# Loading and splitting the expert weights in ten 512 KB pieces, later in the prologue

## The reference, cut to what matters

```python
q, k, v = (split_heads(x @ w.T) for w in (wq, wk, wv))
attn = softmax(where(causal, q @ k.T * 8 ** -0.5, -inf))
x = layernorm(x + (attn @ v) @ wo.T)
coef = route(sigmoid(x @ router_w.T) + e_bias)        # top 4 of 8 groups, top 8 experts
g, u = einsum('th,ehi->tei', x, Wg), einsum('th,ehi->tei', x, Wu)
h = silu(g) * u * coef[:, :, None]
moe = einsum('tei,eih->th', h, Wd)
x = layernorm(x + moe + silu(x @ SWg) * (x @ SWu) @ SWd)
```

## Time and profile before

| | |
|---|---|
| median of three runs | 1035.29 us (1033.92 to 1036.24) |
| the profiled execution | 1035.23 us, of which its span is 1033.2 us |
| PE | 936.0 us busy, 91% of the span |
| DVE, POOL, ACT | 810.7, 626.7, 462.3 us busy (78%, 61%, 45%) |
| mean DMA rate | 117 GB/s over the span; 344 GB/s from 5 to 20 us |
| first matmul of the main loop | 137.41 us |

### The profile page before, as it was taken

How to read it: one execution, slowest core, us unless ns; L and a number is a source line. 1 busy time by engine, 2 the same in 40 slices (tenths; PEclk the granted TensorE clock), 3 DMA queues, 4 the chain that set the end, 5 groups by cost and what they waited for, 6 DMA issues and landing times.

```text
span 1033.2 us, 15722 instructions
## 1 busy us (share of the span) xinstructions
PE 936.0 (91%) x4800; PEld 564.4 (55%) x4800; DVE 810.7 (78%) x2435; ACT 462.3 (45%) x882; POOL 626.7 (61%) x668
## 2 busy tenths in 40 slices
PE   2687699999999899999999899999999999988996
PEld 1233356665566556665566556665566556655653
DVE  5765767798978997799977997798977986587554
ACT  2354345444444444445444444444444545433332
POOL 2432137665676556675676556675676667765775
PEclk7588689999999999999999999999999999999998
DMA  8441153332533253323533253322533232322331
GB/s 297 144 142 49 35 177 109 116 106 103 173 106 116 94 177 110 116 84 124 173 106 116 88 175 118 116 76 103 195 91 116 95 100 83 112 75 84 102 123 51
DMA packets 63075, 120.75 MB, mean 117 GB/s; under 512 B 7056, under 2 KB 34576, under 8 KB 62608
## 3 DMA queue, kind: packets, MB, share of 16 engines
q1 hardware_dynamic: 62992, 119.76, 36.0%
HBM read 97.32 MB, written 22.02 MB: 116 GB/s over the span
## 4 chain that ended last, share of the span: by engine, by line
PE 63%; DVE 27%; issue 4%; DMA 3%; POOL 2%; ACT 1%; SPq 0%; POOLq 0%; DVEq 0%
PE acc L594 8%; DVE max_out L890 7%; PE ob L541 7%; PE sm L511 5%; PE pu L472 5%; PE pg L472 5%; PE st L529 5%; PE pg L474 4%; PE pg L473 4%; PE pu L474 4%; PE pu L473 4%; DVE hid L963 4%; DVE hid L954 3%; PE acc L584 3%; PE acc L586 2%
## 5 line engine op out<-in xcount | busy, mean ns | idle before, releaser
L706 POOL TENSOR_TENSOR hid<-hid,coef_b 128x512 f32<-128x512 f32 x256 | 332.2, 1298 | 197.1 <-DVE hid L963 182.8
L655 ACT ACTIVATE hid<-pg 128x512 f32<-128x512 f32 x264 | 157.7, 597 | 359.9 <-PE pg L474 358.6
L890 DVE CUSTOM_DVE_ANT_0 max_out<-sm,causal_sb 128x128 bf16<-128x128 f32 (+3 forms) x512 | 235.6, 482 | 90.7 <-PE sm L511 89.3
L954 DVE SCALAR_TENSOR_TENSOR hid<-hid,pg 128x512 f32<-128x512 f32 x264 | 180.2, 682 | 86.9 <-ACT hid L655 86.9
L710 POOL TENSOR_TENSOR hid_lo<-hid,hid_hi 128x512 fp32r<-128x512 f32 x128 | 164.2, 1283 | 71.3 <-ACT hid_hi L662 70.0
L627 ACT ACTIVATE probs<-st 128x512 f32<-128x512 f32 (+1 forms) x384 | 187.1, 526 | 20.4 <-PE st L529 18.5
L963 DVE TENSOR_TENSOR hid<-hid,pu 128x512 f32<-128x512 f32 x256 | 174.6, 682 | 10.9 <-PE pu L474 6.2
L511 PE MATMUL sm<-k_stack,q_stack 72*128 72x128 bf16 (+3 forms) x512 | 140.9, 323 | 32.3 <-DMA k_stack<-k_rows_dram 16.5
L692 POOL TENSOR_SCALAR_AFFINE_SELECT probs<-probs 128x256 f32<-128x256 f32 x256 | 102.8, 426 | 75.4 <-ACT probs L627 74.9
L472 PE MATMUL pg<-x_hi,wg_hi 128*128 128x512 f32 x256 | 139.6, 545 | 9.8 <-DVE hid L954 9.7
L472 PE MATMUL pu<-x_hi,wu_hi 128*128 128x512 f32 x256 | 125.0, 488 | 15.7 <-DVE hid L963 15.6
(11 more groups left out here) (129 smaller groups left out, 1213.1 us busy)
## 6 DMA issues: line engine op xcount, KB each, us to landing
coef_b<-coef_dram SPq DMA_DIRECT2D x128, 512.0 KB, 3.9
q_rows_dram<-qk_parts SPq DMA_DIRECT2D x24, 384.0 KB, 3.3
k_rows_dram<-qk_parts SPq DMA_DIRECT2D x24, 384.0 KB, 3.7
q_stack<-q_rows_dram SPq DMA_DIRECT2D x64, 144.0 KB
k_stack<-k_rows_dram SPq DMA_DIRECT2D x64, 144.0 KB
xT_sb<-in_xT SPq DMA_DIRECT2D x8, 256.0 KB, 3.9
y<-in_x SPq DMA_DIRECT2D x8, 256.0 KB, 4.4
out<-out_sb SPq DMA_DIRECT2D x8, 256.0 KB, 2.4
```

Of the source, the lines that this page charges most:

```text
L706: pool.tensor_tensor(hid[:, i % 3, :], hid[:, i % 3, :], coef_b[:, half % 2, j, :], ALU.mult)\
L890: last = dve.tensor_tensor_reduce(out=max_out[:, seg.nth(BANK_SM, task) % 2, col:col + wide], in0=sm_of(seg, task)[:, col:col + wide], in1 ...
L954: dve.scalar_tensor_tensor(hid[:, i % 3, :], hid[:, i % 3, :], 1.0, pg[:, :], ALU.add, ALU.mult).then_inc(a_done, 1)
```

## The change

All weight pieces but SWgu are now quarters of 512 KB and pass through the two halves of coef_b; probs stages nothing any more. The order of the ten is g, u, d, g, u, g, u, d, g, u. Loads stand at places 4.4, 6.1, 7.8 and so on to 21.4, and each split 2.0 places behind its load. DVE computes only the low part of SWgu; POOL does all ten others. wd_sb leaves the group of small weights and is loaded right behind the last piece, with a semaphore that only the first matmul that reads it waits for.

```diff
-SPLIT_BY_DVE = 3
-CHUNKS = 9
+SPLIT_BY_DVE = 1
+CHUNKS = 11
...
-WEIGHT_LOADS = (-4.9, -4.25, -0.25, 2.9, 5.15, 6.8, 8.95, 12.6, 15.45)
-WEIGHT_SPLITS = (-0.09, 2.02, 5.9, 6.7, 9.05, 9.15, 10.1, 15.9, 16.8)
+WEIGHT_LOADS = tuple(4.4 + 1.7 * i for i in range(CHUNKS))
+WEIGHT_SPLITS = tuple(at + 2.0 for at in WEIGHT_LOADS)
...
-        wide, narrow = E * I // 2, E * I // 4
-        waiting = probs[:, :, :].rearrange("p h c -> p (h c)")
+        narrow = E * I // 4
-                  (Wg[:, 0:wide], wg_hi[:, 0:wide], wg_lo[:, 0:wide], waiting[:, 0:wide], 1),
-                  (Wu[:, 0:wide], wu_hi[:, 0:wide], wu_lo[:, 0:wide], waiting[:, wide:2 * wide], 2)]
-        for src, hi, lo, parts in ((Wg, wg_hi, wg_lo, (2, 3)), (Wu, wu_hi, wu_lo, (2, 3)), (Wd, wd_hi, wd_lo, (0, 1))):
+        g, u, d = (Wg, wg_hi, wg_lo), (Wu, wu_hi, wu_lo), (Wd, wd_hi, wd_lo)
+        for (src, hi, lo), part in ((g, 0), (u, 0), (d, 0), (g, 1), (u, 1), (g, 2), (u, 2), (d, 1), (g, 3), (u, 3)):
+            cols, half = slice(part * narrow, (part + 1) * narrow), (len(chunks) - 1) % 2
+            chunks.append((src[:, cols], hi[:, cols], lo[:, cols],
+                           coef_flat[:, half * narrow:(half + 1) * narrow], 1 + half))
...
-                 (sd_sb, SWd), (wd_sb, Wd[:, PAIRS // 2 * D:])]
+                 (sd_sb, SWd)]
...
+                        if i == CHUNKS - 1:
+                            sp.dma_start(wd_sb[:, :], Wd[:, PAIRS // 2 * D:]).then_inc(wd_in, 16)
...
+                            if (n, i) == (0, 2):
+                                pe.wait_ge(wd_in, 16)
```

More of the change, by code:

```diff
@@ L322, in build @@
         wq_in, wkv_in = sem("wq_in"), sem("wkv_in")
-        w_in = sem("w_in")
+        w_in, wd_in = sem("w_in"), sem("wd_in")
         id_in = sem("id_in")
-        split_in = [sem(f"split_in{j}") for j in range(5)]
+        split_in = [sem(f"split_in{j}") for j in range(3)]
         hi_done = sem("hi_done")
@@ L330, in build @@
         const_done = sem("const_done")
-        wide, narrow = E * I // 2, E * I // 4
-        waiting = probs[:, :, :].rearrange("p h c -> p (h c)")
+        narrow = E * I // 4
         coef_flat = coef_b[:, :, :, :].rearrange("p a j t -> p (a j t)")
-        chunks = [(SWgu, sgu_hi[:, :], sgu_lo[:, :], hid[:, 0, 0:2 * P], 0),
-                  (Wg[:, 0:wide], wg_hi[:, 0:wide], wg_lo[:, 0:wide], waiting[:, 0:wide], 1),
-                  (Wu[:, 0:wide], wu_hi[:, 0:wide], wu_lo[:, 0:wide], waiting[:, wide:2 * wide], 2)]
-        for src, hi, lo, parts in ((Wg, wg_hi, wg_lo, (2, 3)), (Wu, wu_hi, wu_lo, (2, 3)), (Wd, wd_hi, wd_lo, (0, 1))):
[L341 to L344, removed]
+        chunks = [(SWgu, sgu_hi[:, :], sgu_lo[:, :], hid[:, 0, 0:2 * P], 0)]
+        g, u, d = (Wg, wg_hi, wg_lo), (Wu, wu_hi, wu_lo), (Wd, wd_hi, wd_lo)
[3 more added lines that the diff above has]
+                           coef_flat[:, half * narrow:(half + 1) * narrow], 1 + half))
         assert len(chunks) == CHUNKS
         small = [(wo_sb, woT), (rw_sb, rwT), (bias_sb, bias.unsqueeze(0).to_broadcast([P, E])),
-                 (sd_sb, SWd), (wd_sb, Wd[:, PAIRS // 2 * D:])]
+                 (sd_sb, SWd)]
         block = ctx.enter_context(nc.Block())
```

## The result

| | before | after |
|---|---|---|
| median of the runs, us | 1034.61 (1033.92 to 1036.24) | 1045.49 (1044.70 to 1046.65) |
| span of the profiled execution, us | 1033.2 | 1043.5 |
| first maxima matmul | 21.14 | 19.57 |
| first `st` | 38.21 | 36.00 |
| second `pv` | 67.47 | 72.19 |

After takes 1.0104 times the time of before, 95% interval 1.0086 to 1.0121: slower by 1%. The row of medians rests on four runs of each kernel. Beside the later experiments, with 16 to 29 runs of before each time, before's median was 1036.6 to 1037.4, and against those the loss would be 8 to 9 us and not 10.9.

The account below looks back on a forecast made before the run. PE bounds the main loop, so its start, set by changing limits in the prologue, decides. Terms -4.1 + 0.4 + 4.5 + 0.3 + 6.5 + 1.1 = +8.7 us on 1035.23 give 1043.9 us, range 1034.5 to 1048.5.

Parts of the forecast that it names:

- rs 1.0: First row load of sequence 1: PE waits for it behind piece 10 and wd_sb; cost 6.5 us (2.4 to 7.2).
- heads 4 to 7: Prologue: POOL's low parts hold the k split and head 7's mask, and rs 0.6 lands later; cost 4.5 us.
- The opening: Start to the first st: weight megabyte off the first rows' path, less DVE work; gain 4.1 us (3.2 to 5.0).
- The rival by which the opening gives only 2 us: Stores limited by something else, so the megabytes stay on the path: 1046 us, inside the range, no chance of its own.
- Heads 0 to 3: Prologue after the first st: low part of piece 4 falls on mn's first step; cost 0.4 us (0 to 1).
- Heads 8 to 11: Prologue: ACT's high part of piece 8 overfills its gap and one st waits; cost 0.3 us.
- The clock: The pv behind the wait for rs 1.0 runs at PE's lower clock; cost 1.1 us (0 to 2.2).
- One for one: Main loop: nothing the change touches runs there, so any prologue gain or loss should pass whole to the end.
- row loads pass the weight loads: Rival at rs 1.0: weight loads don't hold it, PE waits 2.4 us, clock stays up; 1038.7 us, chance 0.10.
- POOL doesn't hold DVE: Rival at heads 4 to 7: cost 2.5 us; with row loads unheld too, 1036.7 us, chance 0.12 for both.
- The early clock: Rival: steadier work gives PE full clock from 38 to 54 us; 1035.7 us, chance 0.08.
- the signs I named: Traces: first st near 34, k split's L865 up to 2.3 us, PE idle about 6 us before sequence 1, among others.

Follow-up runs that it names:

- the kernel before with POOL's wait: Kernel before, with POOL waiting ahead of its third low part until the mn steps of the first four heads are done: 1037.16 us, ratio 0.9988.
- the run with both loads moved: Changed kernel with piece 10 loaded behind row load rs 1.0 and wd_sb behind row load rs 1.1: 1041.97 us, ratio 1.0048.
- SWgu early: Changed kernel with SWgu loaded and split as early as in the kernel before: 1046.40 us, ratio 1.0093 to before.
- POOL's wait on top of it: Changed kernel with SWgu early, POOL waiting ahead of low part 1 for mn of the first four heads, and piece 3 loaded later: 1046.60 us, ratio 1.0087.
- the re-timed kernels: Changed kernel with loads and low parts at other places, wd_sb behind row load rs 1.1: ratios 0.9960 and 0.9973; with POOL also waiting ahead of low part 1, 0.9937.
- wd_sb behind rs 1.1: Kernel before with wd_sb loaded behind the rows of rs 1.1, not ahead of those of rs 0.1: 1037.90 us, ratio 1.0004.
- wd_sb moved: Changed kernel with wd_sb loaded behind row load rs 1.1 instead of ahead of rs 1.0: 1043.17 us, ratio 1.0067 to before.

## Why the prediction was right

The forecast was 1043.9 with 1034.5 to 1048.5; 1045.5 came. The two largest costs, rs 1.0 and heads 4 to 7, stood where they were put and, but for one step of DVE, for the reasons given. That the sum came out only 1.6 us low is in part luck. The main loop began 12.56 us later and not 8.7 (149.97, with 146 forecast), and 2.3 us of that came back inside the main loop, where nothing had been forecast; against the medians of the later runs of before the loss is 8 to 9 us. Nor is the 12.56 sharp: the kernel before with POOL's wait, in which nothing should be slower, began its main loop at 140.54, 3.1 us after before's 137.41. The ends of the terms, as they stand, add up to 1035.4 and 1047.2, not to the 1038 to 1048 written beside them.

**The opening: 2.2 us instead of 4.1.** This is the one term that was badly mis-sized, in three steps. The first row load landed 3.1 us after its issue (16.50 to 19.57), not 2.3. The 2.3 was the time to its last byte, and PE starts later than that: in the run with both loads moved a row load with nothing ahead of it took 2.8 us to PE's start. The small weights behind this one may have cost the rest, which no run shows. SWgu's high part began at 23.40 and not at 22.1. And I let POOL's low part end with the first step of `mn` "as before", 0.48 us: with DVE earlier by 1.7 us and low parts 1 and 2 back to back until 31.74, that step took 1.58. The experiments show the last two as limits side by side: SWgu early gained nothing, and POOL's wait on top of it 2.9 us. The rival by which the opening gives only 2 us was right in its number (1046 forecast, and the nearest of all to the result), though not by its mechanism: the megabyte did leave the path of the first rows. I also expected the stores of k to be issued faster; three took 2.93 us, against 2.92. The price of rs 1.0 leaned on a misreading too: the row load issued at 20.49 stood behind some 2 MB, not 1. The sum itself used the rate, and there that paragraph counts all 2.06 MB.

**Heads 0 to 3: +0.74 for 0.4.** PE waited 0.58 us for rs 0.4, and the first step of `mn` took 1.66 us beside low part 4.

**Heads 4 to 7: +5.6 for 4.5** between the first and second `pv`. DVE lost 2.1 us there, as taken, but at the cast, not at the split's last step, which ran in 0.72. I had used the rule on operations with two SBUF inputs, and had written that one with at most one such input runs on. In the Trainium skill, page "SBUF — State Buffer", section "Who interferes with whom", that second half holds only outside the modes in which DVE uses two ports, and a cast and a tensor_scalar are listed among what can take the port pair that DVE shares with GpSimd. The traces agree: the cast took 2.55 and 0.42 us with and without low part 5 beside it, and `mn`'s first step, a tensor_scalar, 1.77 and 0.17 with and without low parts 1 and 2. I left that condition out and was right in the size only: what held was named wrongly. The rule on two inputs is borne out elsewhere: L908, with two, took 2.24 us beside low part 9. It goes the other way too: in before, POOL's first low part started 0.66 us after DVE's low part of Wu and took 3.83 us instead of 2.35:

```profile
23.36 3.83 POOL L685 TENSOR_TENSOR wg_lo<-coef_b,wg_hi 128x1024 fp32r<-128x1024 f32 x1 [17.78 <-ACT wg_hi L608]
```

PE's wait for rs 0.6 and the mask behind low part 7 are both there.

**Heads 8 to 11: 0.3, and about 0.2 came.** One `st` waited 0.43 us for ACT (79.52), and from the end of the second `pv` to the point where PE stood at rs 1.0 it took 6.35 us against 6.11.

**rs 1.0: 7.14 us for 6.5.** Right in place and cause, and near in size: piece 10 was issued at 81.45, as soon as low part 8 had ended, and the row load took 6.85 us behind 1.5 MB; 6.4 to 6.5 had been taken. What I had noted in passing, that low part 9 "ends inside this wait", turned out to be a second wait of 2.45 us under the first.

**The clock: +1.2 for 1.1.** The `pv` behind the wait took 4.27 us instead of 2.36; the granted clock was 0.58 from 89.6 to 97 us, so mostly the lower of its two levels, 1.2 GHz. The next one took 2.36 instead of 4.15, which gave 1.6 back; this wasn't forecast. The other traces don't make either a law: the fourth `pv` took 4.50 in the re-timed kernels, and the third took 4.49 there, behind a wait of 0.64 us, and 4.50 in the kernel before with POOL's wait, where PE's longest wait since the second `pv` was 0.79. That the long wait is what this `pv` paid for is not shown.

**"One for one": only to about 2 us.** The main loop began 12.56 us later and the span grew by 10.3. In the 14 traces of this study the main loop takes 893.5 to 897.3 us from its first matmul to the end, 895.0 in the mean, whatever the prologue did; before's 895.8 and after's 893.5 both lie in that band. The 2.3 us between them stand in PE's busy time, 844.4 and 841.8 us for the same 4321 instructions. 1.56 of them are one dip of the clock that before's execution had and after's had not, in the same ten matmuls (stretch and length, busy times of PE, PEld, DVE, ACT and POOL, then the clock, DMA share and GB/s, of before and of after):

```profile
242.45:246.45 4.00, 4.00 (x10) 2.55 (x11) 3.93 (x11) 0.00 (x0) 3.41 (x4) 0.57 0.21 71
```

```profile
255.28:257.72 2.44, 2.44 (x10) 1.63 (x11) 2.40 (x8) 0.00 (x0) 2.14 (x3) 1.00 0.33 113
```

**The rivals.** That row loads pass the weight loads fell with PE's wait: 7.14, 4.42 and 0.65 us behind 1.5, 0.5 and 0 MB. That POOL doesn't hold DVE fell with the cast. The early clock fell: from 36 to 54 us it stayed at 0.50 in after. Of the signs I named, the first `st` was to come near 34, and after 36 I would have been wrong; it came at 36.00, on that edge. L865 was to take up to 2.3 us; it took 0.72 (L866 in after), and the cast before it 2.55.

## What to carry to other kernels

A queue is paid for by whoever stands behind: a transfer that waits for a buffer, with a megabyte after it, costs the next urgent load both the wait and the bytes, so put each bulk load right behind the urgent load and not ahead of it, and look which urgent load comes next: wd_sb behind rs 1.1 held rs 1.2. Work moved from DVE to POOL isn't free time: a low part beside a small step that others wait for holds that step for up to its full length, and the same low part beside a `pv` cost next to nothing here. One wait on the right counter brought the first `st` 2.9 us sooner, and the end only where nothing behind it, like the high part of piece 3, stood in the way. When an experiment removes a wait and the work behind it moves by less, look for the wait that it had covered before doubting the price.

## What was not expected of the hardware

- Executions of one program on one core differ in the clock they are granted and in their time together: 16 runs of the kernel before on one core, beside the last experiment, have spans from 1030.7 us at a mean clock of 0.954 to 1038.0 at 0.947. The third `pv` took 2.36 us in the kernel before and 4.50 in the same kernel with POOL's wait, and the first `pv` of the re-timed kernel 2.92 and 2.36 in its two traces.
- The k half of a row load, 144 KB, took 2.8 to 3.6 us from issue to PE's start with nothing queued ahead of it, 4.7 behind 512 KB and 6.85 behind 1.5 MB. So the first 512 KB cost 1.9 us and the megabyte after them 2.2. PE's wait fell by 2.7 with wd_sb moved (7.14 to 4.42), since the row load was also issued 0.6 us sooner relative to PE's coming to it.
- A step of DVE on 128x16 elements, 0.17 us alone, took up to 2.26 us when it began right behind the start of a low part on POOL.
